# Gated cross-attention and fp8 feed-forward on one core: another order of the beginning, and the last batch's rounding and down projection in six pieces

## The chip, the core and the metric

The kernel runs on one core of a Trainium2 chip. The metric is the device time in microseconds (us) of one execution. Three runs of the kernel before took 733.24, 733.21 and 732.18 us; the median is 733.21.

## The reference

For x of 16 batches, 256 tokens and 512 channels, and ctx of 16 x 256 x 128, the block computes (f32 throughout, cut to what matters):

```python
def attention(q, kv, Wq, Wkv, Wout):          # 16 heads of 32 channels
    k, v = jnp.split(kv @ Wkv.T, 2, axis=-1)
    scores = einsum(heads(q @ Wq.T), heads(k)) * 32**-0.5
    attn = softmax(where(causal, scores, finfo.min))
    return merged(attn @ heads(v)) @ Wout.T

def ffn(x, w_gate, w_up, w_down, up_index, down_index):   # 512 -> 1408 -> 512
    qx, sx = rounded_to_fp8(x[:, up_index])    # one scale for each token: max|x| / 448
    g = qlinear(qx, sx, w_gate)[:, down_index] # a weight too: one scale for each row
    u = qlinear(qx, sx, w_up)[:, down_index]
    t = silu(g) * u
    qt, st = rounded_to_fp8(t[:, down_index])
    return qlinear(qt, st, w_down)

x = x + tanh(g_xattn) * attention(layernorm(x), ctx, Wq, Wkv, Wout)
x = x + tanh(g_ffn) * ffn(layernorm(x), ...)
```

## The kernel before, in words

A batch is 256 tokens: two tiles (t = 0, 1) of 128 tokens, tokens on the partitions. The attention's products are computed in bf16 with each operand split into a high and a low part (three products in place of one). The fp8 rounding has no cast: a value is multiplied by the token's factor, an amount that depends on its magnitude is added ("lifted"), and the same amount is taken off again ("rounded"), so that the low bits fall away.

**One batch, step by step.** ScalarE takes means and squares of x (`means1` L2078, `squares1` L2094) and writes the high part and the normalised x (`x_high` L2104, `x_normal` L2114); GpSimd takes the differences (`x_low` L731, `c_low` L722). A transposing DMA brings both to channel-major (`turn_x`, SP's queue). TensorE makes keys, queries and values through the helper `products` (L1163); ScalarE copies them from PSUM as a high part and an exact part (helper `copy`, L1979), and GpSimd writes the low parts (`keys_low` L752, `queries_low` L773). DMAs on SP's queue stack high, high and low parts under each other in K4 and Q4 (`stack_keys`, `stack_queries`), 96 rows, and 29 further rows (96 to 124) hold the row maxima's place and the causal mask as a product. Then scores (L1337), maxima on VectorE (L3052), a second scoring with the maxima taken off (`shifted`), exponentials on ScalarE (L2221), the causal cut on GpSimd (L799), the product with the values, `sums_inverted`, the output projection, the residual and the second normalisation. The feed-forward follows: the token's maximum (`largest_x` L3094), `floored_x`, `lifted_x` (L3131), `rounded_x` (through the helper `low`, L2885), a transposing DMA (`turn_qx`), and then in six chunks n (three for each tile, of 512, 512 and 384 columns) gate and up products, `gate` (VectorE, L3191), `silu` (ScalarE), the up scale (GpSimd, L835) and `up` (VectorE, L3235). For a whole tile of 1408 columns then `largest_t` (L3240), its inverse, `floored_t` (helper L2889), `lifted_t` (L3278), `rounded_t` (L2885), a transposing DMA (`turn_qt`) and 11 products into one PSUM bank (`down`). `down_scaled` (VectorE, L3294) takes it out, `added` (GpSimd, L844) adds it to x, and `store` sends both tiles out.

```python
            def rounded_t(b, t):
                ...
                low(qt[:, t, :], lifted_T[:, t, 0:I], qt[:, t, :]).then_inc(qt_done, 1)
            def turn_qt(b, t):
                ...
                sp.dma_start_transpose(qtT[:, :, tok(t)], qt[:, t, :]).then_inc(qtT_in[t], 16)
```

**Weights.** At the start TensorE turns the weights of the attention (`attention_weights`, n = 0 to 9; 0 and 1 are keys and values, 2 to 5 queries, 6 to 9 output), ScalarE copies each from PSUM twice (a high part in bf16, an exact part in f32) and GpSimd takes the difference. The feed-forward's weights go through in 16 units: 0 to 3 are w_down (128 x 1408 each), 4 to 15 alternate between gate and up (two blocks of 128 x 512). A unit passes `unit_loaded` (SP), `unit_abs` (ScalarE, L2029), `unit_maxima`, `unit_floored`, `unit_lifted` (VectorE, L2996), `unit_rounded`, `unit_turned` (TensorE) and `unit_taken` (ScalarE). VectorE rounds units 3, 1, 0, 2 and 14 (L2885), GpSimd the other eleven (L702). The rows of w_down are put into their order by indirect DMAs through DRAM.

**Order.** There is no scheduler at run time: each engine has its list of steps written out, one call after the other, with waits on semaphores inside the steps, and batches overlap (while batch b is in its attention, b - 1 and b - 2 are in the feed-forward). The middle is five loops `for k in range(1, 9)`, one for each queue (SP L588, GpSimd L976, TensorE L1705, ScalarE L2543, VectorE L3396); the beginning (batches 0 to 2 and the weights) and the end are written out step by step. In the program's names `room` is one block of memory shared by many tiles of the feed-forward and the weights, and `pair` a PSUM pair of banks.

## Time and profile before

| | |
|---|---|
| median of three runs | 733.21 us |
| the profiled execution | 735.42 us |
| its span, first to last instruction | 733.7 us |
| TensorE busy | 664.5 us, 91% |
| VectorE busy | 664.1 us, 91% |
| ScalarE busy | 549.0 us, 75% |
| GpSimd busy | 546.5 us, 74% |
| mean granted TensorE clock | 0.969 |

The span is the time between the first and the last instruction of one execution; the time of the execution has some 1.7 us more around it. The shares are means over stretches that differ: the first 64 us, until the scores of batch 0, hold the preparation of the weights; the rounds of the middle take 38.64 us each; the last 30 us hold the end of batch 15 alone. Steps of the middle are found in the trace by their batch: `sums_inverted` of batch b is used below as the mark of a round.

### The profile page before, as it was taken

To read this page: it belongs to the slowest core of one execution; us is meant where nothing else is said; L and a number is where in the kernel's file an instruction comes from. 1 tells how busy PE (TensorE), PEld (TensorE's weight loads), DVE (VectorE), ACT (ScalarE), POOL (GpSimd) and SP (SyncE) were. 2 spreads that over 40 slices of the span, in tenths; PEclk is the share of its full clock that TensorE was granted. 3 is DMA by queue.
4 is the path that set the end of the run, shared out by engine and by line. 5 is a ranking of instruction groups with operands and counts; after the bars stand their busy time and mean duration, and the time that the engine had idled before them with its cause. 6 is when DMAs were issued, how large, how long until landed. Compare 5 with 4: busy or idle time off the path is not lost.

```text
span 733.7 us, 15607 instructions
## 1 busy us (share of the span) xinstructions
PE 664.5 (91%) x6130; PEld 417.8 (57%) x6130; DVE 664.1 (91%) x1099; ACT 549.0 (75%) x987; POOL 546.5 (74%) x606
## 2 busy tenths in 40 slices
PE   1567889999999999999999999999999999999774
PEld 1456566656666666656565756566666666545331
DVE  5987687999898989999999989999999999899993
ACT  6888768788878796978878787879687868565540
POOL 5777878986868787887878787969597777766551
PEclk9889799999999999999999999999999999999896
DMA  8979875888685749666775757876667664613313
GB/s 308 227 144 201 165 135 99 160 147 158 102 158 92 166 79 195 93 150 110 139 121 136 131 116 143 123 150 112 143 104 147 94 143 76 126 37 78 74 29 96
DMA packets 151207, 95.51 MB, mean 130 GB/s; under 512 B 115326, under 2 KB 121854, under 8 KB 151134
## 3 DMA queue, kind: packets, MB, share of 16 engines
q1 hardware_dynamic: 148974, 92.68, 64.9%
q0 software_dynamic: 576, 1.45, 0.7%
q8 instruction: 48, 0.79, 0.5%
q10 hardware_dynamic: 1584, 0.39, 0.3%
q14 instruction: 25, 0.20, 0.1%
HBM read 31.59 MB, written 9.83 MB: 56 GB/s over the span
## 4 chain that ended last, share of the span: by engine, by line
PE 50%; DVE 24%; ACT 9%; POOL 6%; DMA 5%; issue 2%; SPq 2%; ACTq 0%; POOLq 0%; DVEq 0%
PE pair L1163 30%; PE pair L1401 3%; PE pair L1406 3%; DVE room L2889 3%; PE pair L1432 2%; DVE tm L3240 2%; PE pair L1433 2%; DVE room L3235 2%; POOL PT L799 2%; PE pair L1428 2%; DVE room L2885 2%; DVE mx L3052 2%; DVE room L3278 2%; DVE room L3191 2%; PE pair L1384 1%
## 5 line engine op out<-in xcount | busy, mean ns | idle before, releaser
L835 POOL TENSOR_TENSOR room<-room,up_scale 128x512 f32<-128x512 f32 (+1 forms) x96 | 128.3, 1348 | 38.6 <-ACT room L2303 38.4
L3052 DVE TENSOR_REDUCE mx<-pair 128x6 f32<-128x768 f32 x128 | 116.7, 950 | 4.3 <-PE pair L1339 4.1
L799 POOL TENSOR_SCALAR_AFFINE_SELECT PT<-PT 128x512 f32<-128x512 f32 x128 | 105.6, 854 | 12.4 <-ACT PT L2221 11.7
L2221 ACT ACTIVATE PT<-pair 128x768 f32<-128x768 f32 x128 | 98.0, 816 | 19.3 <-PE pair L1384 16.3
L2303 ACT ACTIVATE room<-room,sx 128x512 f32<-128x512 f32 (+1 forms) x96 | 63.9, 679 | 43.3 <-DVE sx L3156 26.2
L1163 PE MATMUL pair<-WgT,room 128*128 128x512 bf16 (+1 forms) x384 | 91.1, 367 | 4.6 <-DVE room L3235 4.5
L1163 PE MATMUL pair<-WdT,room 128*128 128x512 bf16 x352 | 83.5, 387 | 11.6 <-DMA room<-room 11.6
L1163 PE MATMUL pair<-xT,WqTh 128*128 128x256 bf16 x512 | 88.5, 276 | 4.0 <-ACT x L1979 4.0
L1163 PE MATMUL pair<-WuT,room 128*128 128x512 bf16 (+1 forms) x384 | 91.6, 364 | 0.1
L1163 PE MATMUL pair<-xT,WqTl 128*128 128x256 bf16 x256 | 70.5, 276 | 0.0
L3235 DVE TENSOR_TENSOR room<-pair,room 128x512 f32<-128x512 f32 (+1 forms) x96 | 60.7, 636 | 9.8 <-POOL x L844 6.5
L1163 PEld LDWEIGHTS pair<-WdT,room 128*128 128x128 bf16 x352 | 34.5, 99 | 54.4 <-DMA room<-room 13.7
L731 POOL TENSOR_TENSOR xcat<-xin,xcat 128x512 bf16<-128x512 f32 x32 | 38.0, 1192 | 33.4 <-ACT xin L2114 33.3
L3191 DVE TENSOR_TENSOR room<-pair,gate_scale 128x512 f32<-128x512 f32 (+1 forms) x96 | 59.6, 637 | 1.9 <-PE pair L1163 0.8
L844 POOL TENSOR_TENSOR x<-room,x 128x512 f32<-128x512 f32 x32 | 43.4, 1356 | 21.9 <-DVE room L3294 21.8
L1979 ACT ACTIVATE exact<-pair 128x512 f32<-128x512 f32 x64 | 37.9, 594 | 27.7 <-PE pair L1163 19.7
L1163 PEld LDWEIGHTS pair<-WgT,room 128*128 128x128 bf16 x384 | 36.8, 99 | 38.2 <-issue 7.2
L1163 PEld LDWEIGHTS pair<-xT,WqTh 128*128 128x128 bf16 x512 | 49.9, 99 | 14.7 <-ACT x L1979 4.2
L3278 DVE SCALAR_TENSOR_TENSOR room<-room,tmult 128x1408 f16<-128x1408 f32 x32 | 58.0, 1812 | 0.1
L2333 ACT ACTIVATE room<-room 128x512 bf16<-128x512 f32 (+1 forms) x96 | 54.0, 582 | 4.5 <-DVE room L3235 4.5
L1401 PE MATMUL pair<-PT,V 128*32 128x256 f32 (+1 forms) x1024 | 55.6, 336 | 1.2 <-POOL PT L799 0.8
L1337 PE MATMUL pair<-K,Q 125*128 125x128 bf16 x256 | 49.6, 220 | 5.9 <-DMA Q<-kl 1.5
(137 smaller groups left out, 1854.4 us busy)
## 6 DMA issues: line engine op xcount, KB each, us to landing
xin<-in_x_dram SPq DMA_DIRECT2D x16, 512.0 KB, 4.8
x<-in_x_dram SPq DMA_DIRECT2D x16, 512.0 KB, 3.9
K<-kh SPq DMA_DIRECT2D x32, 256.0 KB, 5.7
Q<-qh SPq DMA_DIRECT2D x32, 256.0 KB, 4.9
out_dram<-x SPq DMA_DIRECT2D x16, 512.0 KB, 3.2
K<-kl SPq DMA_DIRECT2D x16, 256.0 KB, 6.8
Q<-kl SPq DMA_DIRECT2D x16, 256.0 KB, 4.9
room<-in_L_ffn_w_down_dram SPq DMA_DIRECT2D x4, 704.0 KB, 8.0
```

What stands on the lines that cost most here:

```text
L799: pool.affine_select(out=view, in_=view, compare_op=ALU.is_ge, fill=0.0, base=0, pattern=[[0, 2], [0, 2], [1, P]], channel_multiplier=-1). ...
L835: pool.tensor_tensor(g, g, up_scale[:, chunk(n)[1]], ALU.mult).then_inc(slw_done, 1)
L1163: last = pe.matmul(out_ap, lhs, rhs, start=(fresh and n == 0), stop=(n == len(terms) - 1), skip_group_check=not fresh)
L1337: pe.matmul(w[:, tok(4 * h)], q[0:MASK_END, head, 0:P], k[0:MASK_END, head, 0:P], start=True, stop=True)
L1401: pe.matmul(w[HD * j:HD * j + HD, t * P:S], V[:, t, (G * g + j) * HD:(G * g + j + 1) * HD], probabilities(b, 2 * g + j // 2, j % 2, t), st ...
L2221: act.activation(head_columns(ring(b, c), 0, 384), head_columns(shifted_pair[c][:, :], 0, 384), ACT.Exp, scale=SCALE).then_inc(exp_done, 1)
L2303: act.activation(g, g, ACT.Silu, scale=sx[:, chunk(n)[0]:chunk(n)[0] + 1]).then_inc(silu_done, 1)
L2333: act.activation(qt[:, t, f], T[:, t, f], ACT.Abs, scale=TOKEN_LIFT).then_inc(abst_done, 1)
L3052: dve.tensor_reduce(mx[:, heads, :], head_columns(w, 0, 3 * P).rearrange("p h (r s) -> p h r s", s=P), AX.X, ALU.max).then_inc(max_done, 1)
L3191: dve.tensor_tensor(gs[:, n % 3, 0:width(n)], gate_bank[n][:, 0:width(n)], gate_scale[:, f], ALU.mult).then_inc(gs_done, 1)
L3235: dve.tensor_tensor(T[:, t, f], up_bank[n][:, 0:width(n)], gs[:, n % 3, 0:width(n)], ALU.mult).then_inc(t_done, 1)
L3278: dve.scalar_tensor_tensor(out=lifted_T[:, t, 0:I], in0=T[:, t, :], scalar=tmult[:, t:t + 1], in1=qt[:, t, :], op0=ALU.mult, op1=ALU.add). ...
```

## The change

The lists of all five queues are written anew. What is computed stays. The parts:

- **Loads.** The context and x of batch 0 are loaded ahead of units 1, 2 and 3 of w_down; the output weights after the first transposing DMAs.
- **Weights of keys and queries.** TensorE turns them with an identity matrix whose columns are read in another order (`by_place`), so that ScalarE's copies need no strided view.
- **Mask rows.** Rows 96 to 124 of Q4 and K4 are written by four copies on VectorE (`put_queries`, `put_keys`) from tiles that GpSimd builds on 128 partitions. Eight DMAs (`mask_of_queries`, `mask_of_keys`, `keys_ones`, and `no_maxima` of batches 0 and 1) go.
- **Rounding of the weights.** VectorE rounds units 0 to 4, 6, 8, 10, 12 and 14; GpSimd 5, 7, 9, 11, 13 and 15, and none of them ahead of `queries_low` of batch 0.
- **PSUM banks and orders** in the beginning, the middle and the end, with the waits that follow from them.
- **Batch 15.** x is turned by TensorE (`turned_x`) and copied out by ScalarE in place of `turn_qx`. Maximum, flooring, lifting and rounding of t go in the six chunks; each chunk is turned by TensorE (`turned_t`), copied out by ScalarE and multiplied at once (`down_part`). The second tile is added on VectorE (`added_last`), and the two tiles are stored by a DMA each.

```diff
 # SP
             load_w_kv()
-            unit_loaded(3)
-            unit_loaded(2)
-            unit_loaded(1)
+            load_c(0)
             unit_loaded(0)
             load_x(0)
-            load_c(0)
+            unit_loaded(1)
+            unit_loaded(2)
+            unit_loaded(3)
             load_w_q()
+            load_x1(0)
+            load_c(1)
+            turn_x(0, 0)
+            load_x(1)
+            turn_x(0, 1)
             load_w_out()
-            mask_of_queries(0)
...
+            def store_half(b, t):
+                if t == 0 and b == 15:
+                    sp.wait_ge(o_added, 31)
+                if t == 1 and b == 15:
+                    sp.wait_ge(o_added_last, 1)
+                sp.dma_start(out[b][tok(t), :], x1[b % NX][:, t, :]).then_inc(stored, 16)
...
-            turn_qt(15, 0)
-            turn_qt(15, 1)
             store(14)
-            store(15)
-            sp.wait_ge(stored, 16 * NB)
+            store_half(15, 0)
+            store_half(15, 1)
+            sp.wait_ge(stored, 16 * NB + 16)
 # TensorE
+            by_place = ident[:, :].rearrange("p (j c) -> p c j", j=G)
...
-                    last = pe.transpose(bank[aw_bank[n]][:, m * P:(m + 1) * P], src, ident[:, :])
+                    last = pe.transpose(bank[aw_bank[n]][:, m * P:(m + 1) * P], src, ident[:, :] if n == 1 or n >= 6 else by_place)
...
+            def turned_x(b, t):
+                if b == 15:
+                    pe.wait_ge(qx_done, t + 31)
+                for kk in range(KT):
+                    last = pe.transpose(turned_x_room(t)[:, tok(kk)], qx[:, t, tok(kk)], identb[:, :])
+                last.then_inc(tx_made, 1)
+
+            def turned_t(b, n):
+                if b == 15:
+                    pe.wait_ge(qt_part, n + 1)
+                if n == 5 and b == 15:
+                    pe.wait_ge(tt_taken, 5)
+                t, f = chunk(n)
+                for m in range(width(n) // P):
+                    last = pe.transpose(turned_room(n)[:, tok(m)], qt[:, t, f][:, tok(m)], identb[:, :])
+                last.then_inc(tt_made, 1)
+
+            def down_part(b, n):
...
+                t, here = chunk(n)[0], blocks(n)
+                for i in range(here.start, here.stop):
+                    last = pe.matmul(down_bank[t], qtT[:, i, tok(t)], WdT[:, i, :], start=(i == 0), stop=(i == IT - 1),
+                                     skip_group_check=True)
...
-            down(15, 0)
-            down(15, 1)
+            turned_t(15, 0)
+            turned_t(15, 1)
+            down_part(15, 0)
+            turned_t(15, 2)
+            down_part(15, 1)
+            turned_t(15, 3)
+            down_part(15, 2)
+            turned_t(15, 4)
+            down_part(15, 3)
+            turned_t(15, 5)
+            down_part(15, 4)
+            down_part(15, 5)
 # ScalarE
+            def turned_t_taken(b, n):
+                if b == 15:
+                    act.wait_ge(tt_made, n + 1)
+                copy(qtT[:, blocks(n), tok(chunk(n)[0])], turned_room(n).rearrange("p (k s) -> p k s", s=P)).then_inc(tt_taken, 1)
 # VectorE
+            def put_queries(i):
+                if i == 0:
+                    dve.wait_ge(const, N_CONST)
+                dve.tensor_copy(Q4[i][96:MASK_END, :, :].rearrange("r h (t s) -> r (h t) s", t=TT),
+                                rows_q[96:MASK_END, None, :].to_broadcast([MASK_END - 96, NH * TT, P])).then_inc(q_put, 1)
...
+                dve.tensor_reduce(tm_parts[:, n:n + 1], T[:, t, f], AX.X, ALU.max, apply_absolute_value=True).then_inc(tpart_done, 1)
...
+                dve.tensor_reduce(tm[:, t:t + 1], tm_parts[:, CF * t:CF * t + CF], AX.X, ALU.max).then_inc(tjoin_done, 1)
...
+                dve.tensor_tensor(x1[b % NX][:, t, :], T[:, t, 0:H], x1[b % NX][:, t, :], ALU.add).then_inc(o_added_last, 1)
...
             down_scaled(14, 1)
+            largest_joined(15, 0)
             gate(15, 5)
-            largest_t(15, 0)
+            largest_t_inverted(15, 0)
+            floored_part(15, 0)
+            floored_part(15, 1)
             up(15, 3)
             up(15, 4)
+            lifted_part(15, 0)
+            floored_part(15, 2)
             up(15, 5)
-            largest_t_inverted(15, 0)
-            largest_t(15, 1)
-            floored_t(15, 0)
+            lifted_part(15, 1)
+            rounded_part(15, 0)
+            largest_part(15, 3)
+            largest_part(15, 4)
+            largest_part(15, 5)
+            rounded_part(15, 1)
+            largest_joined(15, 1)
+            lifted_part(15, 2)
             largest_t_inverted(15, 1)
-            lifted_t(15, 0)
-            floored_t(15, 1)
-            rounded_t(15, 0)
-            lifted_t(15, 1)
-            rounded_t(15, 1)
+            rounded_part(15, 2)
+            floored_part(15, 3)
+            lifted_part(15, 3)
+            floored_part(15, 4)
+            rounded_part(15, 3)
+            lifted_part(15, 4)
+            rounded_part(15, 4)
+            floored_part(15, 5)
+            lifted_part(15, 5)
+            rounded_part(15, 5)
             down_scaled(15, 0)
             down_scaled(15, 1)
+            added_last(15, 1)
```

ScalarE's list ahead of the exact copy of the queries of batch 0 loses six copies of the output weights, one `unit_taken` of w_down, one of a gate unit and two `unit_abs`; behind that copy and ahead of `x_normal(1, 1)` stands one `unit_abs`. On GpSimd `x_low(1, 1)` and `queries_low(0, 1)` follow each other without a rounding between. On SP `turn_x(1, 0)` stands ahead of `stack_queries(0, 1)`.

## Rows read from the trace of the kernel before

**Rows 1.** Table of windows: start:end and length in us, busy us (instructions) by engine, clock, DMA
```profile
0.00:63.99 63.99, 30.46 (x216) 24.77 (x217) 49.20 (x66) 51.80 (x79) 42.63 (x56) 0.89 0.85 213
63.99:93.92 29.93, 25.40 (x294) 18.39 (x295) 22.77 (x37) 22.73 (x39) 25.94 (x29) 0.83 0.90 192
93.92:127.77 33.85, 30.86 (x343) 21.87 (x342) 26.49 (x50) 27.60 (x51) 25.74 (x33) 0.95 0.62 118
...
282.72:321.36 38.64, 38.64 (x371) 24.39 (x370) 36.44 (x64) 31.31 (x59) 30.79 (x34) 1.00 0.71 131
...
668.52:703.00 34.48, 29.16 (x127) 12.65 (x126) 34.02 (x63) 15.17 (x28) 17.62 (x14) 0.90 0.27 59
703.00:733.70 30.70, 14.69 (x59) 6.05 (x57) 16.98 (x24) 6.33 (x12) 10.27 (x9) 0.82 0.25 65
```

The columns of rows 1 are, after the stretch and its length, the busy us of PE, PEld, DVE, ACT and POOL with the number of instructions, the granted TensorE clock as a share, the DMA share and GB/s. The stretches end at the first scores, at `sums_inverted` of batches 0 and 1, after a full round, and at the end.

**Rows 2.** Groups of instructions by form, ScalarE, first 64 us: xcount | busy, mean ns | idle before
```profile
L1979 ACT ACTIVATE WdT<-pair 128x1408 bf16<-128x1408 bf16 x4 | 5.4, 1360 | 2.3 <-PE pair L1219 2.3
L1979 ACT ACTIVATE WqTh<-pair 128x512 bf16<-128x512 f32 x4 | 5.1, 1343 | 0.0
L2114 ACT ACTIVATE xin<-xin,shift,rstd 128x512 f32<-128x512 f32 x4 | 3.3, 814 | 0.1
...
L1979 ACT ACTIVATE WoTh<-pair 128x512 bf16<-128x512 f32 x4 | 2.4, 602 | 0.0
```

**Rows 3.** Timeline up to the first scores: start, duration in us, engine, line, tiles
```profile
57.23 0.59 ACT L1979 ACTIVATE exact<-pair 128x512 f32<-128x512 f32 x1
...
57.89 1.16 POOL L773 TENSOR_TENSOR kl<-exact,qh 128x512 bf16<-128x512 f32 x1
...
63.99 0.22 PE L1337 MATMUL pair<-K,Q 125*128 125x128 bf16 x1 [1.31 <-DMA Q<-kl]
```

**Rows 4.** Groups of instructions by form, GpSimd, first 64 us
```profile
L702 POOL TENSOR_TENSOR room<-room 128x1024 bf16<-128x1024 f32 x4 | 9.0, 2260 | 1.3 <-DVE room L2996 1.3
```

**Rows 5.** Groups of instructions by form, VectorE, first 130 us
```profile
L2996 DVE SCALAR_TENSOR_TENSOR room<-room,wmult 128x512 f32<-128x512 f32 x22 | 20.0, 959 | 0.1
...
L2889 DVE TENSOR_SCALAR room<-room,wmult 128x1408 bf16<-128x1408 bf16 x4 | 2.2, 582 | 0.1
...
L2885 DVE TENSOR_TENSOR room<-room 128x1024 bf16<-128x1024 f32 x1 | 1.2, 1214 | 0.0
```

**Rows 6.** Timeline of the end
```profile
698.07 0.42 DVE L2885 TENSOR_TENSOR room<-cx,room 128x512 bf16<-128x512 f16 x1
...
701.72 0.75 DVE L3294 SCALAR_TENSOR_TENSOR room<-pair,st,down_scale 128x512 f32<-128x512 f32 x1
702.39 0.55 DVE L3191 TENSOR_TENSOR room<-pair,gate_scale 128x384 f32<-128x384 f32 x1
703.85 0.69 DVE L3235 TENSOR_TENSOR room<-pair,room 128x512 f32<-128x512 f32 x1 [0.91 <-POOL x L844]
...
708.01 0.55 DVE L3191 TENSOR_TENSOR room<-pair,gate_scale 128x384 f32<-128x384 f32 x1
...
718.92 0.89 DVE L2885 TENSOR_TENSOR room<-room 128x1408 bf16<-128x1408 f16 x1
...
720.94 7.37 PE L1163 MATMUL pair<-WdT,room 128*128 128x512 bf16 x22 [10.62 <-DMA room<-room]
...
729.18 1.26 POOL L844 TENSOR_TENSOR x<-room,x 128x512 f32<-128x512 f32 x1 [1.23 <-DVE room L3294]
```

**Rows 7.** Groups of instructions by form, VectorE, from 640 us on
```profile
L3131 DVE SCALAR_TENSOR_TENSOR cx<-cx,xmult,room 128x512 f16<-128x512 f32 x4 | 3.1, 766 | 0.0
...
L3094 DVE TENSOR_REDUCE amax<-cx 128x1 f32<-128x512 f32 x4 | 2.6, 673 | 0.0
...
L2889 DVE TENSOR_SCALAR room<-room,xmult 128x512 bf16<-128x512 bf16 x4 | 1.3, 344 | 0.0
```

**Rows 8.** The chain that ended last, from 704 us on
```profile
720.94 4.89 PE pair L1163 x11
```

**Rows 9.** The page's list of DMA issues: count, KB each, median us to landing
```profile
Q<-kl SPq DMA_DIRECT2D x16, 256.0 KB, 4.9
```

More of the change, by code:

```diff
@@ new lines, in _ @@
+            for k in range(1, 9):
+                stack_keys(k + 4, 0)
+                stack_keys(k + 4, 1)
+                stack_keys(k + 4, 2)
+                turn_qt(k, 1)
+                load_c(k + 5)
+                stack_queries(k + 4, 0)
+                store(k)
+                stack_queries(k + 4, 1)
+                turn_qt(k + 1, 0)
+                turn_qx(k + 2, 0)
+                stack_queries(k + 4, 2)
+                load_x1(k + 3)
+                turn_x(k + 5, 0)
+                turn_x(k + 5, 1)
+                load_x(k + 6)
+                turn_qx(k + 2, 1)
+                no_maxima(k + 5)
@@ new lines, in _ @@
+            load_c(14)
+            stack_keys(13, 0)
+            stack_keys(13, 1)
+            stack_keys(13, 2)
+            turn_qt(9, 1)
+            stack_queries(13, 0)
+            load_c(15)
+            stack_queries(13, 1)
+            stack_queries(13, 2)
+            store(9)
+            turn_qt(10, 0)
+            turn_qx(11, 0)
+            no_maxima(14)
+            load_x1(12)
+            turn_x(14, 0)
+            turn_x(14, 1)
+            load_x(15)
+            turn_qx(11, 1)
@@ L606, in _ @@
+            turn_qt(10, 1)
+            stack_keys(14, 0)
+            stack_queries(14, 0)
+            stack_keys(14, 1)
+            stack_keys(14, 2)
+            stack_queries(14, 1)
+            turn_qt(11, 0)
+            store(10)
+            turn_qx(12, 0)
             stack_queries(14, 2)
-            turn_qx(12, 0)
-            turn_qt(11, 0)
             load_x1(13)
@@ L1113, in _ @@
             causal_part(14, 7)
[L1114 to L1116 removed]
+            up_scaled(12, 5)
             added(12, 0)
@@ L2383, in _ @@
+            c_high(1)
+            keys_exact(0, 1)
             keys_high(0, 1)
+            means1(1, 1)
+            squares1(1, 1)
+            values_taken(0, 0)
+            unit_taken(2)
             attention_weights_high(9)
             unit_taken(0)
-            means1(1, 0)
+            unit_taken(1)
             attention_weights_exact(9)
-            keys_exact(0, 1)
+            x_high(1, 0)
+            queries_high(0, 0)
+            unit_abs(4)
+            x_normal(1, 0)
+            x_high(1, 1)
@@ L2480, in _ @@
             centred(0, 0)
-            abs_x(0, 0)
-            unit_taken(12)
-            squares2(0, 0)
+            x_high(3, 0)
+            x_normal(3, 0)
+            x_high(3, 1)
+            exps(1, 0)
+            unit_abs(15)
+            exps(1, 1)
+            queries_high(2, 1)
+            exps(1, 2)
             queries_exact(2, 1)
-            queries_high(2, 1)
-            exps(1, 0)
-            exps(1, 1)
-            exps(1, 2)
             exps(1, 3)
@@ new lines, in _ @@
+            silu(1, 0)
+            keys_high(4, 1)
+            abs_t(0, 5)
+            silu(1, 1)
+            means1(5, 0)
+            squares1(5, 0)
+            centred(2, 0)
+            means1(5, 1)
+            squares1(5, 1)
+            abs_t(1, 0)
+            silu(1, 2)
+            maxima_taken(3)
+            queries_high(4, 0)
+            abs_x(2, 0)
+            silu(1, 3)
+            maxima_sent(3)
+            silu(1, 4)
+            abs_t(1, 1)
+            abs_t(1, 2)
+            queries_exact(4, 0)
@@ new lines, in _ @@
+            maxima(2, 5)
+            gate(0, 0)
+            scale_x(0)
+            lifted_x(0, 1)
+            maxima(2, 6)
+            rounded_x(0, 1)
+            gate(0, 1)
+            maxima(2, 7)
+            second_maxima(2)
+            largest_x(1, 0)
+            up(0, 0)
+            gate(0, 2)
+            up(0, 1)
+            gate(0, 3)
+            gate(0, 4)
+            up(0, 2)
+            largest_t(0, 0)
+            largest_t_inverted(0, 0)
+            floored_t(0, 0)
@@ new lines, in _ @@
+            residual(1, 1)
+            lifted_t(0, 0)
+            gate(0, 5)
+            up(0, 3)
+            largest_x(1, 1)
+            largest_x_inverted(1)
+            floored_x(1, 0)
+            floored_x(1, 1)
+            lifted_x(1, 0)
+            rounded_t(0, 0)
+            rounded_x(1, 0)
+            up(0, 4)
+            up(0, 5)
+            largest_t(0, 1)
+            sums_inverted(2)
+            inverse_spread(2, 0)
+            inverse_spread(2, 1)
+            normalised(2, 0)
```

3216 lines of the change are left out of this document (1601 added, 1615 removed).

## The prediction

> **What bounds the kernel now.** I read the table of windows first. In a round of the middle PE is busy 38.64 of 38.64 us and VectorE 36.44 [rows 1]: there PE sets the pace, and the instructions of a round are what they were. In the first 63.99 us, until the first scores, no engine is full: PE 30.46, VectorE 49.20, ScalarE 51.80, GpSimd 42.63 [rows 1]. That stretch is a chain of waits with the weights' preparation threaded through it. Between 63.99 and 127.77 VectorE stands idle for 29.93 - 22.77 + 33.85 - 26.49 = 14.5 us. At the end VectorE is busy 34.02 of 34.48 us up to 703, so its work alone decides when the last batch's products come; after 703 it is busy 16.98 of 30.70 and PE 14.69 [rows 1]: a chain with one engine at a time. So there are two places where order can win, and a middle where it can only lose.
>
> **The beginning.** The change puts batch 0's context and x before three of the four w_down units on the load queue, and thins out what stands on ScalarE in front of queries_exact(0, 1). Before, that copy starts at 57.23; its difference on GpSimd ends at 57.89 + 1.16 = 59.05; the first scores wait for its stacking transfer until 63.99 [rows 3], and the median landing of such a transfer is 4.9 us [rows 9]. Counting the two ScalarE queues up to that copy, the new one has left out six copies of Wo's parts (6 x 0.60), one unit_taken of w_down (1.36 for 1408 columns), one of a gate unit and two unit_abs (1024 columns, by that rate 1.0 each): 8.0 us [rows 2]. Five high parts of Wq and Wk were written with a stride and took 1.34 on average against 0.60 for the plain ones [rows 2]; the turned identity gives the order instead, which saves 5 x 0.74 = 3.7. The copy then starts at 57.2 - 11.7 = 45.5 and ends at 46.1. Behind it stand one unit_abs (1.0) and x_normal(1, 1) (0.81) [rows 2], then on GpSimd x_low(1, 1) and queries_low(0, 1), about 1.2 each: 50.3. GpSimd is free for them, because four roundings of 2.26 [rows 4], 9.0 us that stood in front, are now on VectorE or behind. With 4.9 for the transfer the first scores come at 55.2, **8.8 earlier**. On SP two waits are in front of that transfer: turn_x(1, 0) needs values(0, 1) and x_low(1, 0), and behind it are queued stack_queries(0, 1) and (0, 2), for which the scores wait; both conditions are met some us before 50.3 in the same count, so I charge nothing, and each us that values(0, 1) is later than that is one for the scores. Reading the identity with a stride costs PE something no row shows; PE is idle half of the stretch, so nothing.
>
> Part of this is paid back. Five weight units more are rounded by VectorE: 1.21 each [rows 5]. Four copies of 29 x 4096 bf16 now write the mask rows; eight small transfers disappear from SP's queue. No row shows such a copy. From below: 1408 bf16 elements take 0.58 [rows 5], at that rate 4096 take 1.7. From above: the difference of two inputs takes 1.21 for 1024 [rows 5], so 4.8. The copy is nearest to the first row in type and operands, and I take 1.7. Of the Trainium skill, "VectorE: DVE Perf Modes", the perf-mode tier table, gives 0.69 us for a bf16 copy of 2048 elements within SBUF and 2.29 for an operation held to one element a cycle; worked out from it, an estimate is 1.3 for 4096, by which the sum would be 0.4 lower than by the row, and 4.6 if the copy falls to the slow form. No run so far shows which. Two of the four, the copies for batch 0, lie in the wait for w_down and x; the third and the roundings 4 and 6 are before the first scores, and adding VectorE's queue up by rows it is there at about 53, ahead of 55.2. After the scores come roundings 8, 10 and 12 (3.6), the last copy (1.7) and the unit_lifted(7) that used to be earlier (some 1.4 to 1.9 with two tiles of 0.96 [rows 5]): 6.9 us of new work against 14.5 of idle time, with ScalarE's 8.0 us coming there too. Idle time comes in pieces, so I take it that 60% is absorbed and **2.7 is paid** (bounds 0 and 6.9). The beginning gives 8.8 - 2.7 = **6.1**, between 1.9 and 8.8.
>
> **The middle.** Other banks, another interleaving, some waits fewer and some new. Each new wait that I followed (scores(b, 1) on the values' copies, down(b, 1) on a query copy) has at least 2.4 us of PE work between its producer's start and itself. Cost nothing; the cover is PE's own queue, and if it is gone, a round gets longer by the wait.
>
> **The end.** Let G be the end of gate(15, 5), 708.01 + 0.55 = 708.56 [rows 6]. Before, VectorE's last rounding ends at 718.92 + 0.89 = 719.81, 11.25 after G. From there to the end of the span it is 13.9 us: a transposing transfer, 22 products of 512 columns, scaling, GpSimd's addition of 1.26 and the store [rows 6].
>
> In the pieces, starts follow each other some 0.08 sooner than the durations, as at 701.72, 0.75 and the next at 702.39 [rows 6]. So a floored piece of 512 costs 0.26, a lifted 0.69, a maximum 0.59 [rows 7], a rounded 0.34 [rows 6], those of 384 about 0.22, 0.55, 0.47 and 0.28. Behind G in the new order stand three up (1.67), six floored (1.48), six lifted (3.86), six rounded (1.92), three maxima (1.65) and the joins and inverses (0.5): 11.1, with waits for one's own results 11.5. In front of G stand three maxima and a join, 1.8 in all, of which the 0.91 of idle time in front of 703.85 [rows 6] takes some: G moves by 1.2 (0.7 to 1.8).
>
> PE gets its first product about 7 after G. By G + 11.5, at 0.44 each (4.89 for 11 [rows 8]) and with the transposes between, it has done 8 or 9 of 22. The other 13 or 14 cost 0.225 each if the clock has come up, as it did in before for the second 11: (7.37 - 4.89) / 11 [rows 6, 8]; with the last copy out of PSUM 3.6 (bounds 2.2, full clock throughout and 7 products left, and 6.7). Then scaling 0.75 and a wait, 0.8; the addition on VectorE 0.7, as the other operation with two inputs of 512 [rows 7], instead of GpSimd's 1.26; the store, 3.26 for both halves before (from 730.44 to 733.7), 2.8 for one half. In all 7.9 behind the last rounding. **Gain 13.9 - 7.9 - 1.2 - 0.2 = 4.6**, between 1.5 and 6.0. That x of batch 15 is turned by PE gains nothing: its next user waits on VectorE, full until 703. The other half's addition and store lie beside PE's second half.
>
> **The rivals.**
> - *VectorE pays all* (14%). All 6.9 is paid; the beginning gives 1.9. For: its 36.44 of 38.64 leaves little in the round after. Against: 14.5 idle. Time 722.5 + 4.2 = 726.7.
> - *The last products stay at half clock* (7%). For: between up(15, 5) and the first piece PE is idle for 2 us and then stops and goes, and it began at 0.44 after the pause until 720.94 [rows 8]. Against: its products are back to back from G + 7. Time 722.5 + 3.1 = 725.6. The Trainium skill, "TensorE: Matmul & The Clock Gate", Part 1, has the rule that an idle array falls to 1.2 GHz and goes back to 2.4 only after sustained activity. The two halves of batch 15's products in the trace agree with it; by it the time would lie between the forecast and this rival.
> - *The mask copies run one element at a time* (8%), ending slower. 4.8 instead of 1.7 each, on a queue that every weight must pass, and none of it absorbed: 12.4 more, 734.9; it decides from 1.7 + 10.7 / 4 = 4.4 us a copy. For: the source repeats 128 elements 32 times, which no row has. Against: bf16 to bf16 within SBUF, as the 0.58 row.
> - *A new wait in each round* (5%). At 1.07 us in ten rounds nothing would be left: 733.2. For: PE has no slack. Against: no wait followed above is uncovered.
> - *Nothing is paid back* (4%): all of 14.5 is usable; 719.8.
>
> **How the numbers follow.** The profiled execution took 735.4, its span 733.7; the median of the runs shown is 733.2, 2.2 less. 735.4 - 6.1 - 4.6 = 724.7, and less 2.2 is **722.5**, the likeliest case (62%). With both ends at their best it is 735.4 - 14.8 - 2.2 = 718.4, at their worst 735.4 - 3.4 - 2.2 = 729.8; a little of the middle on either side makes the range 715 to 731. Runs differ by 0.15%, so 0.2% (1.5 us) is what can be told from no change. Faster 62 + 14 + 7 + 4 + 1 = 88%, same 4%, slower 8%.
>
> **What would show it.** In the new trace: first scores at 54 to 57; the four mask copies at 1.2 to 2 us; batch 2's sums_inverted 4 to 8 us earlier; a round still at 38.6; the last rounding some 1.4 later than before, relative to the beginning's shift; products of the last piece at 0.22; the last store 8 us behind the last rounding. The forecast is wrong if the scores come early and the first full round doesn't, or if a round is over 39 us.

## The result and the profile after

| | before | after |
|---|---|---|
| median (lowest to highest), us | 733.10 (732.18 to 733.24) | 728.88 (727.30 to 729.82) |
| profiled execution / its span, us | 735.42 / 733.7 | 729.19 / 727.4 |
| mean granted clock | 0.969 | 0.978 |

The ratio is 0.9938, with a 95% interval of 0.9921 to 0.9956: 4.2 us faster where 10.7 were forecast. The time lies inside the range, far from the likeliest case.

The span falls into five stretches at marks that both kernels have: the start of the inverse of batch 1's sums (`sums_inverted(1)`), the same of batch 12, the end of `gate(15, 5)` (G), the end of the last rounding (R), and the last store.

| us | to `sums_inverted(1)` | to `sums_inverted(12)` | to G | G to R | R to the end |
|---|---|---|---|---|---|
| before | 127.8 | 426.8 | 154.0 | 11.3 | 13.9 |
| after | 121.6 | 426.7 | 159.9 | 12.7 | 6.6 |
| forecast of the change | -6.1 | 0 | +1.2 | +0.2 | -6.0 |
| measured between the two traces | -6.1 | -0.1 | **+5.9** | +1.4 | -7.3 |

The first two come out as forecast. The last two are 1.2 and 1.3 off, one against the other. The third, with the last whole batches, gives 5.9 us back, 4.7 more than forecast. The table of windows of the changed kernel (start:end, length, then busy us and instructions of PE, PEld, DVE, ACT, POOL, clock, DMA share, GB/s) has these stretches in finer cuts; its first cut, 55.72, is the first maxima on the scores, 1.0 us behind the first scores:

```profile
0.00:55.72 55.72, 28.16 (x192) 23.42 (x195) 45.33 (x55) 44.93 (x74) 38.33 (x54) 0.89 0.84 228
55.72:86.59 30.87, 24.18 (x303) 18.59 (x304) 30.63 (x47) 23.28 (x39) 26.27 (x27) 0.92 0.71 177
86.59:121.63 35.04, 30.03 (x335) 21.54 (x337) 31.38 (x56) 28.18 (x51) 32.63 (x35) 0.95 0.78 154
...
277.19:317.08 39.89, 38.31 (x365) 24.51 (x369) 36.67 (x62) 31.80 (x59) 30.08 (x35) 1.00 0.65 126
317.08:355.55 38.47, 38.15 (x365) 24.54 (x369) 36.77 (x63) 31.70 (x59) 29.96 (x35) 1.00 0.69 130
...
548.30:708.16 159.86, 147.62 (x1199) 82.48 (x1213) 154.30 (x263) 103.19 (x183) 102.80 (x109) 0.99 0.45 85
708.16:727.40 19.24, 9.27 (x49) 4.43 (x48) 14.49 (x32) 5.90 (x12) 3.09 (x3) 0.79 0.14 55
```

The same view of the kernel before, for the two last stretches:

```profile
554.58:708.56 153.98, 145.89 (x1203) 82.77 (x1202) 147.72 (x257) 100.64 (x179) 103.96 (x107) 0.98 0.47 92
708.56:733.70 25.14, 9.13 (x32) 3.31 (x29) 12.62 (x17) 3.26 (x7) 4.93 (x5) 0.78 0.26 71
```

Three things are to be seen. From 55.72 to 86.59 VectorE is now busy 30.63 of 30.87 us, where it had 7 us of idle time in the second stretch of [rows 1]. A full round is 38.47 against 38.64. And from batch 12's sums to G VectorE does six instructions more but is busy 154.30 instead of 147.72 us, 6.6 us more, while its idle time is 5.6 instead of 6.3: it is not waits that grew, single steps have become longer. The groups of VectorE by form in that stretch say which. Before, and then after (count | busy us, mean ns):

```profile
L3131 DVE SCALAR_TENSOR_TENSOR cx<-cx,xmult,room 128x512 f16<-128x512 f32 x8 | 6.7, 839 | 0.1
...
L2889 DVE TENSOR_SCALAR room<-room,xmult 128x512 bf16<-128x512 bf16 x8 | 3.2, 413 | 0.0
...
L3156 DVE SCALAR_TENSOR_TENSOR sx<-amax,rstd 128x2 f32<-128x2 f32 x4 | 0.6, 153 | 0.0
```

```profile
L3198 DVE SCALAR_TENSOR_TENSOR cx<-cx,xmult,room 128x512 f16<-128x512 f32 x9 | 9.3, 1031 | 0.0
...
L2947 DVE TENSOR_SCALAR room<-room,xmult 128x512 bf16<-128x512 bf16 x8 | 5.3, 658 | 0.0
...
L3217 DVE SCALAR_TENSOR_TENSOR sx<-amax,rstd 128x2 f32<-128x2 f32 x5 | 1.9, 376 | 0.0
```

`lifted_x` goes from 839 to 1031 ns, `floored_x` from 413 to 658, and `scale_x`, two elements a partition, from 153 to 376. Eight microseconds of the changed kernel's timeline (start, duration, engine, line) show how:

```profile
582.44 1.00 POOL L832 TENSOR_TENSOR room<-room,up_scale 128x384 f32<-128x384 f32 x1
582.47 1.13 DVE L2947 TENSOR_SCALAR room<-room,xmult 128x512 bf16<-128x512 bf16 x1
...
584.02 1.21 DVE L3198 SCALAR_TENSOR_TENSOR cx<-cx,xmult,room 128x512 f16<-128x512 f32 x1
...
584.65 2.92 POOL L765 TENSOR_TENSOR kl<-exact,qh 128x512 bf16<-128x512 f32 x2
...
585.26 1.27 DVE L2943 TENSOR_TENSOR room<-cx,room 128x512 bf16<-128x512 f16 x1
...
588.15 1.17 POOL L729 TENSOR_TENSOR xcat<-xin,xcat 128x512 bf16<-128x512 f32 x1
...
588.37 1.10 DVE L2947 TENSOR_SCALAR room<-room,xmult 128x512 bf16<-128x512 bf16 x1
```

A floored step of 0.34 us in [rows 7] takes 1.13 when it starts 0.03 after a GpSimd step of 1.00, and 1.10 beside one of 1.17; a rounding of 0.42 in [rows 6] takes 1.27 beside two differences. In the traces of both kernels, every VectorE step of this stretch that is longer than the shortest of its kind by over 0.15 us has a GpSimd step beside it. Added up over the stretch, these excesses are 5.2 us before and 10.1 after, and the same in a second trace of each kernel. GpSimd is busy two thirds of the stretch, so the neighbourhood alone proves little; the experiments below test it.

The end, in the timeline of the changed kernel:

```profile
707.61 0.55 DVE L3260 TENSOR_TENSOR room<-pair,gate_scale 128x384 f32<-128x384 f32 x1
...
708.53 1.64 DVE L2947 TENSOR_SCALAR room<-room,tmult 128x512 bf16<-128x512 bf16 x2
...
709.02 0.99 POOL L832 TENSOR_TENSOR room<-room,up_scale 128x384 f32<-128x384 f32 x1
...
716.15 1.91 PE L1554 MATMUL pair<-WdT,room 128*128 128x512 bf16 x4
...
720.50 0.36 DVE L2943 TENSOR_TENSOR room<-room 128x384 bf16<-128x384 f16 x1
...
721.78 1.67 PE L1554 MATMUL pair<-WdT,room 128*128 128x512 bf16 x7
...
723.49 0.75 DVE L3447 SCALAR_TENSOR_TENSOR room<-pair,st,down_scale 128x512 f32<-128x512 f32 x1 [1.97 <-PE pair L1554]
724.27 0.69 DVE L3453 TENSOR_TENSOR x<-room,x 128x512 f32<-128x512 f32 x1
```

When the last rounding ends at 720.86, PE has begun 11 or 12 of the 22 products (the trace has records of 21). The last seven take 1.67 us; the last of them lasts 0.38 by itself, so their starts follow each other by some 0.22. The two floored pieces at 708.53 take 1.64 instead of some 0.6, beside GpSimd's last scaling.

### The profile page after: what moved, and what is told of

Read it like the earlier page. It is cut to its first block, busy times and chain, and to the rows that moved or that the text cites. A ratio compares the mean times of both kernels' runs of the same rounds, so it can differ in the third digit from the quotient of the medians.

```text
span 727.4 us, 15637 instructions
## 1 busy us (share of the span) xinstructions
PE 657.9 (90%) x6091; PEld 419.9 (58%) x6160; DVE 680.1 (93%) x1127; ACT 555.5 (76%) x995; POOL 538.5 (74%) x601
## 4 chain that ended last, share of the span: by engine, by line
PE 47%; DVE 29%; POOL 11%; DMA 5%; issue 3%; ACT 3%; SPq 0%; ACTq 0%; DVEq 0%
PE pair L1153 26%; DVE mx L3116 5%; POOL PT L793 4%; PE pair L1411 4%; PE pair L1416 3%; DVE room L2943 2%; DVE room L2947 2%; PE pair L1394 2%; DVE room L3260 2%; PE pair L1440 2%; DVE room L3308 2%; PE pair L1436 2%; POOL room L832 2%; DVE tm L3323 2%; DVE wmax L2962 2%
## 5 line engine op out<-in xcount | busy, mean ns | idle before, releaser
L832 POOL TENSOR_TENSOR room<-room,up_scale 128x512 f32<-128x512 f32 (+1 forms) x96 | 125.6, 1312 | 63.1 <-ACT room L2349 62.2
L1153 PE MATMUL pair<-xT,WqTh 128*128 128x256 bf16 x512 | 86.5, 272 | 1.5 <-ACT WdT L2037 1.3
L1153 PE MATMUL pair<-WuT,room 128*128 128x512 bf16 (+1 forms) x368 | 84.8, 361 | 3.3 <-DVE room L3260 1.4
L1153 PE MATMUL pair<-WdT,room 128*128 128x512 bf16 x326 | 75.4, 379 | 3.1 <-DMA room<-room 2.9
L2381 ACT ACTIVATE room<-room 128x512 bf16<-128x512 f32 (+1 forms) x96 | 55.8, 586 | 21.2 <-DVE room L3308 21.1
L1153 PEld LDWEIGHTS pair<-WuT,room 128*128 128x128 bf16 x384 | 36.9, 98 | 35.1 <-DVE room L3260 2.0
L1341 PE MATMUL pair<-K,Q 125*128 125x128 bf16 x256 | 51.4, 224 | 6.1 <-DMA Q<-kl 3.6
L2943 DVE TENSOR_TENSOR room<-room 128x1408 bf16<-128x1408 f16 (+4 forms) x46 | 55.4, 1205 | 0.2
L1153 PEld LDWEIGHTS pair<-WdT,room 128*128 128x128 bf16 x330 | 31.7, 98 | 40.3 <-issue 2.9
L1416 PE MATMUL pair<-PT,pick 128*32 128x256 f32 (+1 forms) x1024 | 53.5, 326 | 0.0
```

The lines of the kernel that those rows point to most:

```text
L832: pool.tensor_tensor(g, g, up_scale[:, chunk(n)[1]], ALU.mult).then_inc(slw_done, 1)
L1153: last = pe.matmul(out_ap, lhs, rhs, start=(fresh and n == 0), stop=(n == len(terms) - 1), skip_group_check=not fresh)
L1416: last = pe.matmul(sum_bank[HD * j:HD * j + HD, t * P:S], pick[:, g, :], probabilities(b, 2 * g + j // 2, j % 2, t), start=(g == 0 and t = ...
L2381: act.activation(qt[:, t, f], T[:, t, f], ACT.Abs, scale=TOKEN_LIFT).then_inc(abst_done, 1)
L2943: return dve.tensor_tensor(dst, w, high, ALU.subtract)
```

## The experiments

**What the pieces at the end are worth.** In `e2_whole_end` batch 15 goes by whole tiles, with GpSimd's addition and one store, as before; the rest of the change stays (x of batch 15 still turned by PE). `e1_after_again` is the changed kernel once more, run beside it.

```diff
-            turned_t(15, 0)
-            turned_t(15, 1)
-            down_part(15, 0)
...
-            down_part(15, 5)
+            down(15, 0)
+            down(15, 1)
...
-            abs_t(15, 0)
             silu(15, 3)
+            abs_t(15, 0)
```

> The changed kernel unchanged, for a second trace and as the base of this series. The prediction took 2.2 us off because the profiled execution of the kernel before was that much above its median; the profiled execution of the changed kernel is only 0.3 above its own. If the 1.1 and 1.4 us by which two rounds of the middle stretched (199.19 to 238.72 and 277.19 to 317.08) are a matter of one execution, they are elsewhere or gone here, and the time stays within 1.5 us of 728.9. If they belong to the order, they come again in the same two rounds.

> Only the end of batch 15 is undone: maxima, rounding, turning and down products of t for whole tiles, with the two transposing DMAs, GpSimd's addition and one store, as before; all else as changed. Theory: in the two profiles the end of the last gate step lies at 708.56 and 708.16, and from there to the end it is 25.14 us before and 19.24 after, so the pieces give 5.9 less the 1.2 us or more that the three early maxima cost ahead of it: this kernel is 4 to 6 us slower than the changed one, some 733.5, so that the whole gain of the change would be its end. Rival: the gain of the beginning is there too, and the end is worth only half: 2 to 3 us slower, some 731.5.

Measured: 729.24 and 732.23 us beside 733.75 for the kernel before; ratios 0.9926 (0.9902 to 0.9949) and 0.9975 (0.9962 to 0.9988). The pieces are worth 3.0 us: the rival's 2 to 3 came out, not the 4 to 6. In the traces G to the end is 25.46 with whole tiles and 19.28 (19.4 to 20.3 in the two repeats) in pieces, 5.2 to 6.2 less; 0.8 is paid ahead of G, and the other 1.4 to 2.4 are within the scatter of the beginning and the rounds. From batch 12's sums to G it is 159.06, so the pieces aren't what lengthens that stretch.

**Whether GpSimd's work lengthens it.** `e3_little_gpsimd_before` and `e4_little_gpsimd_after` are the two kernels with four kinds of GpSimd steps of the last batches cut to a few columns: the up scale and the last addition, shown here, and the causal cut and the low part of the normalised output. They leave out the rest of these steps' work.

```diff
-                pool.tensor_tensor(g, g, up_scale[:, chunk(n)[1]], ALU.mult).then_inc(slw_done, 1)
+                few = width(n) if b < 11 else 16
+                pool.tensor_tensor(g[:, 0:few], g[:, 0:few], up_scale[:, chunk(n)[1]][:, 0:few], ALU.mult).then_inc(slw_done, 1)
...
-                pool.tensor_tensor(x1[b % NX][:, t, :], T[:, t, 0:H], x1[b % NX][:, t, :], ALU.add).then_inc(o_added, 1)
+                few = H if b < 11 else 16
+                pool.tensor_tensor(x1[b % NX][:, t, 0:few], T[:, t, 0:few], x1[b % NX][:, t, 0:few], ALU.add).then_inc(o_added, 1)
```

> The kernel before with GpSimd's large steps of the last batches cut to a few columns: the causal cut and the low part of the normalised output from batch 12 on, the up scale and the last addition from batch 11 on. The rest of these steps is left out. Theory: VectorE's steps that read SBUF twice, or write two-byte results from SBUF, last longer while GpSimd works: between 549 and 711 us of the profile their durations lie 7.7 us above the shortest ones of their kind before, 14.1 us after the change, and that is what ate the gain. Without GpSimd's work both kernels lose these, and as PE bounds part of the stretch, the kernel before gets 3 to 6 us faster. Rival: the gain was lost to the order of steps and its waits; then the two kernels gain the same.

> The changed kernel with the same steps of GpSimd cut to a few columns. Theory of the held-up VectorE steps: this kernel gains 7 to 11 us, so that the distance of the two is 8 to 11 us here, where it is 4.2 with GpSimd's work. Rival, order and waits: it gains as much as the kernel before does, and the distance stays 4 to 6.

Measured: 733.43 (ratio 0.9996, 0.9981 to 1.0012), no change for the kernel before, where 3 to 6 us were expected, and 721.42 (0.9835, 0.9809 to 0.9861) for the changed one, 7.8 less than in `e1_after_again`. The windows from batch 12's sums to G, first of the kernel before, then of the changed one:

```profile
551.95:705.84 153.89, 144.84 (x1203) 82.61 (x1202) 144.00 (x257) 100.28 (x178) 50.67 (x108) 0.99 0.49 92
```

```profile
546.26:700.95 154.69, 145.84 (x1213) 82.71 (x1212) 146.75 (x263) 101.52 (x181) 45.89 (x109) 1.00 0.47 88
```

With GpSimd out of the way the two orders need 153.9 and 154.7, and of the second 0.8 is the pieces' early maxima: they are equal. In the kernel before, VectorE's busy time falls by 3.7 us and its idle time rises by 3.6: the hold-ups fell into its waits. In the changed kernel the busy time falls by 7.5 and the stretch by 5.2.

**Reads or writes.** That experiment also brought GpSimd's results earlier. `e5_writes_only` keeps GpSimd nearly as busy, but replaces the same steps by fills of their own outputs, which read nothing. It was tried on the changed kernel alone.

```diff
+                if b >= 11:
+                    pool.memset(bytes_of(g)[:, 0:width(n) * 11 // 4], 60).then_inc(slw_done, 1)
+                    return
                 pool.tensor_tensor(g, g, up_scale[:, chunk(n)[1]], ALU.mult).then_inc(slw_done, 1)
```

> The changed kernel; the same steps of GpSimd as in the run before (causal cut and low part of the normalised output from batch 12 on, up scale and last addition from batch 11 on) are not left out but replaced by plain fills of their output, counted in bytes so that they take about as long: by the profile a fill of 128 elements takes 0.205 us and a tiny one 0.10, so an estimate for 1408 is 1.25, as the up scale has. So GpSimd stays as busy and its steps keep their place in the chain, but they read nothing. Theory: what holds VectorE's steps is that both read SBUF; the ones with two inputs are free, the time falls to 721 to 725, and the held-up time between 549 and 711 us falls from 14.1 to under 8. Rival: the 7.8 us of the last run came from the shorter chain of gate, up scale and up; then this kernel takes 728 to 730.

Measured: 725.68 us, ratio 0.9882 (0.9852 to 0.9913), just above the theory's 721 to 725. The stretch and three of its groups:

```profile
547.36:704.16 156.80, 147.63 (x1215) 83.25 (x1213) 149.61 (x263) 101.76 (x182) 91.05 (x109) 0.99 0.46 87
```

```profile
L3213 DVE SCALAR_TENSOR_TENSOR cx<-cx,xmult,room 128x512 f16<-128x512 f32 x9 | 6.7, 741 | 0.0
...
L2962 DVE TENSOR_SCALAR room<-room,tmult 128x1408 bf16<-128x1408 bf16 x9 | 7.6, 848 | 0.0
...
L2962 DVE TENSOR_SCALAR room<-room,xmult 128x512 bf16<-128x512 bf16 x8 | 3.9, 491 | 0.0
```

GpSimd is busy 91 us here against 102.8, and the stretch is 3.1 us shorter. `lifted_x`, with two inputs in SBUF, falls to 741 ns, the value it has with GpSimd cut (745). The floored steps, with one input of two-byte values, are not freed: that of x falls only to 491 (440 with GpSimd cut), and that of t, 1408 columns, rises to 848, from 593 in the changed kernel and 589 with GpSimd cut. Steps with two inputs that are still over 0.15 us longer than the shortest of their kind lie beside a GpSimd step that still reads (two of them); four floored steps of t, 0.25 to 0.74 longer, have nothing but fills beside them. The timeline has one floored pair held by a fill:

```profile
704.53 1.64 DVE L2962 TENSOR_SCALAR room<-room,tmult 128x512 bf16<-128x512 bf16 x2
...
705.01 1.02 POOL L842 MEMSET room<- 128x1056 uint8 x1
```

So steps are held by what GpSimd does in SBUF, and not only moved by the time at which its results come: in these runs two-input steps wait for its reads, two-byte floored steps for its writes too.

**Whether the order can avoid it.** `e13_moved_six` moves six VectorE steps of batches 12 to 15 out of the way of GpSimd steps (with one wait that the new order needs); `e7_moved` has a seventh, `down_scaled(13, 0)` ahead of `lifted_x(14, 1)`. `e14_after_third` is the changed kernel, run beside `e13_moved_six`.

```diff
-            floored_x(12, 1)
             sums_inverted(13)
+            floored_x(12, 1)
...
-            scale_x(12)
             maxima(14, 2)
             maxima(14, 3)
+            scale_x(12)
             lifted_x(12, 1)
+            rounded_x(12, 1)
             residual(13, 0)
             maxima(14, 4)
             maxima(14, 5)
-            rounded_x(12, 1)
...
-            floored_part(15, 1)
             up(15, 3)
+            floored_part(15, 1)
```

> The changed kernel with seven held-up VectorE steps of the last batches moved by a place or two in VectorE's list, so that they don't begin beside a reading GpSimd step, and nothing else: scale_x(12) behind two maxima, rounded_x(12, 1) ahead of residual(13, 0), floored_x(12, 1) behind sums_inverted(13), up(12, 3) ahead of floored_x(13, 0), gate(13, 3) ahead of rounded_t(12, 1), down_scaled(13, 0) ahead of lifted_x(14, 1), up(15, 3) ahead of floored_part(15, 1). Their held-up times add to 5.1 us in the profile (0.75, 0.72, 0.76, 0.58, 0.62, 0.91, 0.76). Theory: each move saves what its step waited, unless the next one is held instead: 2 to 4 us faster than the changed kernel, 725 to 727. Rival, it is not these waits that set the end: within 0.7 us of it.

> The changed kernel with six of the seven moves of held-up VectorE steps, without down_scaled(13, 0), which let GpSimd's addition of batch 13 start earlier and hold lifted_t(13, 1) for 1.0 us. From the profile of the seven: 1.0 us back behind sums_inverted of batch 15, lifted_x(14, 1) held for 0.9 again. So 1.5 to 2.5 us faster than the changed kernel of the same call. Rival, the order of these steps does not set the end: within 0.7 us of it.

> The changed kernel unchanged, on the same chip as the run before, as its base: 728 to 730.

Measured: 727.59 with seven, 725.92 with six (0.9900, 0.9882 to 0.9918), 728.68 for the changed kernel beside it. The seventh move brought GpSimd's `added(13, 0)` forward onto `lifted_t(13, 1)`, which it held for 1.02 us. With six the stretch is

```profile
546.92:705.34 158.42, 147.00 (x1199) 82.76 (x1213) 152.61 (x263) 102.95 (x183) 102.08 (x109) 0.99 0.47 86
```

and G to R falls from 12.70 to 12.10. That is the fastest version that computes everything, 7.8 us below the kernel before. Most of the 10.1 us of excess stays (8.6), as other steps come to lie beside GpSimd steps: a floored tile of t is now 0.77 us longer than the shortest. The fall of 1.5 us in the excess and of 1.4 in the stretch go together.

**What VectorE's extra work at the beginning costs.** `e6_more_puts` makes the third and the fourth mask copy three times each.

```diff
             put_queries(1)
+            put_queries(1)
+            put_queries(1)
...
             put_keys(1)
+            put_keys(1)
+            put_keys(1)
```

> The changed kernel with four more mask copies of 1.22 us on VectorE: two more of the queries' rows ahead of the first scores and two more of the keys' rows behind them, 4.9 us of work. The prediction took 60% of new VectorE work after the first scores as absorbed in idle time. By it this kernel is 1 to 2.5 us slower than the changed one. Rival: VectorE was idle 0.2, 0.2, 1.4 and 0.7 us in the four stretches of 20 us from 40 to 120, so it is the bound there and all 4.9 is paid. Second rival: nothing is paid, since TensorE sets the end of that stretch.

Measured: 736.27 us (1.0031, 1.0013 to 1.0049), 7.0 more than the changed kernel. The timeline has the copies of the third mask, and those of the fourth:

```profile
39.86 4.94 DVE L2957 COPY Q<-rows_q 29x4096 bf16<-29x4096 bf16 x3
...
78.79 4.71 DVE L2964 COPY K<-rows_k 29x4096 bf16<-29x4096 bf16 x3
```

In the changed kernel the single copies take 1.22 and 1.56 us. So the four more are not the 4.9 us of work that was expected of them but 3.7 + 3.2 = 6.9: beside GpSimd steps they too take longer, and each us of work costs 1.0 us, not the 1.4 that the next expectation takes from it. The first scores' maxima come 3.4 later than after, batch 1's sums 7.8 later. Nothing is absorbed.

**The mask rows by transfers instead.** `e9_mask_dma` takes the four copies off VectorE, as four DMAs from SP; `e11_mask_dma_split` splits each into 3 and 26 partitions and puts them at other places. `e10_mask_dma_moved` and `e12_split_moved` add the six moves. The lines are those of `e11_mask_dma_split`:

```diff
+            def mask_rows(into, rows, i):
+                for first, last in ((96, MASK_START), (MASK_START, MASK_END)):
+                    sp.dma_start(into[i][first:last, :, :].rearrange("r h (t s) -> r (h t) s", t=TT),
+                                 rows[first:last, None, :].to_broadcast([last - first, NH * TT, P])).then_inc(mask_in[i], 16)
...
-            put_queries(0)
-            put_keys(0)
```

> The changed kernel with the mask rows written by four DMAs of SP's queue, from the tiles that GpSimd builds now, in place of the four copies on VectorE; nothing else differs. In the run with four copies more, each us of VectorE work in the beginning cost 1.4 us of the whole (7.0 for 4.9). Theory, VectorE is the bound of the beginning: without the 5.2 us of the four copies the kernel is 3 to 7 us faster than the changed one, 722 to 726. Rival: the first two copies lie in the wait for the weights and the other two are paid back by the transfers, which the first scores now wait for: within 1 us of 729.2.

> The same, and six of the seven moves of held-up steps; the seventh, down_scaled(13, 0) ahead of lifted_x(14, 1), is left out, since it let GpSimd's addition of batch 13 start earlier and hold lifted_t(13, 1) for 1.0 us. Theory: both gains add, 1.6 us and a little more behind the run with the mask DMAs alone, some 722. Rival: an earlier beginning shifts which steps meet, and the moves are worth nothing: the same as the mask DMAs alone.

> The mask rows by DMAs again, but each copy of 29 partitions as two, of 3 and of 26, as in the kernel before, and the four of a pair no longer one behind the other on the queue. In the run before, a copy of 29 partitions went out at some 142 packets in 2 us, 13 us for its 928, and the loads behind it waited 45 us in all; in the kernel before, 832 packets of 26 partitions went out in about 4 us. Theory, VectorE is the bound of the beginning and the 29 partitions were the fault: 3 to 7 us faster than the changed kernel, 722 to 726. Rival, any such transfer of 256-byte pieces holds the loads up: slower than the changed kernel.

> The same with the six moves of held-up steps. In the two runs before, the stretch from sums_inverted of batch 1 to the end was 604.4 without the moves and 603.6 with them, against 605.8 of the changed kernel: expected are 1 to 2 us less than in the run with the split DMAs alone, some 721 to 724. Rival: the moves are worth nothing, the same time.

Measured: 774.8 us with the four DMAs, 731.81 with the split ones, and 771.5 and 728.55 with the six moves added. All four were expected between 721 and 726. In `e9_mask_dma` the next issues on SP's queue stand still (timeline of the queue):

```profile
23.28 0.85 SPq L457 DMA_DIRECT2D Q<-rows_q  x1
24.17 15.48 SPq L459 DMA_DIRECT2D K<-rows_k  x1
39.69 13.01 SPq L366 DMA_DIRECT2D room<-in_L_ffn_w_gate_dram  x1
```

and all that is behind them is late: batch 1's sums come at 167.68. Split, the kernel is still some 3 us slower than with the copies: batch 1's sums come at 124.74, and loads behind the transfers on SP's queue are issued later (the first unit's at 25.34 instead of 24.43, the fourth's at 41.95 instead of 37.90). As far as these two forms go, the copies on VectorE were the better choice.

**The kernel before, once more**, in `e8_before_again`.

> The kernel before unchanged, for a second trace. In its first profile sums_inverted of batch 1 is at 127.77; in the run with GpSimd's steps cut, whose beginning is the same code, it is at 125.33. If the 2.2 us by which the profiled execution lay over its median are the beginning's scatter, the mark comes at 124 to 128 here, and from it to the end it is 606 again. If the scatter is elsewhere, the mark is at 127.8 and the rest differs.

Measured: 734.13 in one execution, its span 732.4: G to the end 24.46, and 153.59 from batch 12's sums to G.

## Why the prediction was right and where it was wrong

**The failed step** is the one on the last whole batches: that G moves by 1.2 us, as three maxima and a join in front of it less some idle time, and that the changed interleaving of batches 12 to 15 costs nothing, with PE's queue as cover. The first half was right by itself: those four take 2.04 us after, and `sums_inverted(15)` to G, 43.04 after and 42.27 with whole tiles, makes them worth 0.8. The second half failed, because VectorE's durations were taken from [rows 6, 7] as fixed. They aren't fixed, and the trace of before shows it already: the floored step, 0.34 in [rows 7], has a mean of 0.41 over the whole stretch. Near the end VectorE had little idle time (34.02 of 34.48 us busy in the prediction's own rows, PE 29.16), so longer steps moved G. The excess beside GpSimd went from 5.2 to 10.1 us, and G by 5.9: 4.7 more than forecast. Of the 5.9, 5.2 go with GpSimd's work (`e4_little_gpsimd_after`); 3.1 go when it reads nothing (`e5_writes_only`), where it is also 12 us less busy. The other 2.1 can be its writes, or its results coming later than with little work; the runs don't part these.

The Trainium skill, "SBUF — State Buffer", section "Who interferes with whom", has this rule: VectorE shares its second pair of SBUF ports with GpSimd, and a step with two SBUF inputs contends with GpSimd's reads, a step in a two-port mode with GpSimd whatever it does; the first to issue has the pair for its whole instruction. The runs agree: 741 ns for two inputs beside fills and 1031 beside reads, and 1.64 us for a floored pair beside a fill. Here it was up to about 1 us a step, and 10.1 us in a stretch of 160.

**The beginning.** The first scores come at 54.69 (forecast 55.2), the exact copy starts at 44.51 (45.5), and `queries_low(0, 1)` ends at 49.49 + 1.20 = 50.69 (50.3). In the changed kernel's timeline:

```profile
44.51 0.65 ACT L2037 ACTIVATE exact<-pair 128x512 f32<-128x512 f32 x1
...
49.49 1.20 POOL L765 TENSOR_TENSOR kl<-exact,qh 128x512 bf16<-128x512 f32 x1
...
54.69 0.29 PE L1341 MATMUL pair<-K,Q 125*128 125x128 bf16 x1 [2.02 <-DMA Q<-kl]
```

A mask copy takes 1.22 us (the last 1.56, beside GpSimd): under the lower bound of 1.7 that was scaled from 1408 elements in [rows 5]; that row's rate doesn't carry over to 4096. The estimate from the Trainium skill, "VectorE: DVE Perf Modes", the perf-mode tier table, was 1.3, and the trace agrees. The sum of 6.1 was met, 6.1 between the two profiles, but by luck. The first scores came 9.3 earlier, not 8.8. Between them and batch 1's sums VectorE is busy 63.04 us after and 49.26 before: 13.8 us of new work where 6.9 were counted, since five liftings of weight tiles and two maxima now come behind the earlier scores and the roundings there take 1.57 us each instead of 1.21. Of the 13.8 only 3.2 was paid, so more was absorbed than the 60% that were taken without a ground; and with it the idle time of the first part is used up (30.63 of 30.87 us), which is why `e6_more_puts` pays for all of its copies. The kernel before has its mark of batch 1's sums at 125.3, 127.3 and 127.8 in three traces (the first that of `e3_little_gpsimd_before`), the changed one between 120.5 and 122.2, so the gain is some 4 to 6 rather than exactly 6.

**The rounds** cost nothing, as forecast: 426.7 us over eleven of them against 426.8.

**The end.** G to the end was to be 11.5 + 7.9 = 19.4, and is 19.28 (20.30 and 19.42 in the repeats). Both parts are off, one against the other: to R 12.70, since a floored pair was held for 1.0 us (11.67 in `e4_little_gpsimd_after`), and from R 6.58, since PE had 10 or 11 products left and not 13 or 14, and the store took 2.5 and not 2.8. The last products followed each other by 0.22, as forecast. In `e1_after_again`, where the granted clock is 0.50 (1.2 GHz) from 715 to 720.7, R to the end is 7.60.

**The 2.2 us taken off** the profiled time belonged to that one execution of the kernel before; the changed kernel's profile is 0.3 above its median. So 1.9 of the gain between the two profiles is not in the medians. With the 4.7 of the failed step that closes the sum: 722.5 + 4.7 + 1.9 = 729.1, against 728.9.

**The rivals.** "VectorE pays all" was the nearest, with 726.7: VectorE does pay at the beginning, but the loss that decided is in the last whole batches and from another cause. The half clock was partly there: after PE had waited 4.59 us for the first rounded piece the granted clock is 0.50 (1.2 GHz) from 715 to 719, but it is 1.00 (2.4 GHz) from 720 to 723.5, and the last seven products are there. Slow mask copies (1.22) and a new wait in each round (38.47) are refuted. The range held because the bounds of the two ends reached to 729.8, not because a bound of the failed step did.

## What to carry to other kernels

A VectorE step's duration depends on what GpSimd does beside it, and where VectorE sets the pace that sets the time. Here a step with two inputs in SBUF went from 0.73 to 1.64 us, and a two-byte floored step from 0.34 to 1.13. So a changed order is to be costed with the pairs that it makes, and an order is tuned for these pairs even when nobody wrote that down. Compare the mean duration of the same group in both traces before looking for a new wait: busy time that rises by more than the added instructions is the sign. A test that cuts the neighbour's work in both kernels tells what the order itself costs.

## What was not expected of the hardware

- In `e9_mask_dma` a transfer of 29 partitions in 32 pieces of 256 bytes took some 13 us, its 928 packets going out at about 142 in 2 us, and the queue that had issued it stood for 15.48 and 13.01 us; 26 partitions, 832 packets, took some 4 us in the kernel before.
- One round of the changed kernel takes 39.89 us, in every trace of that order, where its neighbours take 38.5: between batch 5's and batch 6's sums PE waits 1.27 us for a transposing transfer that lands some 5.7 us after its issue, where the same transfer of the rounds before and after lands after some 3.6. In PE's timeline:

```profile
304.53 1.67 PE L1153 MATMUL pair<-WdT,room 128*128 128x512 bf16 x7 [1.27 <-DMA room<-room]
```

What that transfer collides with wasn't tried and stays open. The other long round of the first trace, 39.53 us from 199.19, is 38.46 in both repeats, so it belonged to that execution.
